# Graph layer 0: VectorE adds runs of equal targets before TensorE sums them per group

## The reference

```python
h = relu(layernorm(x))                                   # layer 0
agg = segment_sum(h[src], dst, 12500)
x = x + agg @ W_rel.T + b_rel + h @ W_root.T
h = relu(layernorm(x))                                   # layer 1
w = silu(edge_attr @ We1 + be1) @ We2 + be2              # 50 -> 128 -> 128 per edge
agg = segment_sum(h[src] * w, dst, 12500)
x = x + silu(agg @ Wn1 + bn1) @ Wn2 + bn2 + h
```

## Time and profile before

| | us |
|---|---|
| median of 3 runs | 4800.75 (4791.8 to 4805.88) |
| profiled execution | 4849.66, its span 4847.9 |
| POOL busy | 2970.8 (61%) |
| TensorE busy | 2418.4 (50%) |
| VectorE busy | 1276.0 (26%) |
| ScalarE busy | 479.4 (10%) |

### The profile page before, as it was taken

How to read it: one execution, slowest core, us unless ns; L and a number is a source line. 1 busy time by engine, 2 the same in 40 slices (tenths; PEclk the granted TensorE clock), 3 DMA queues, 4 the chain that set the end, 5 groups by cost and what they waited for, 6 DMA issues and landing times.

```text
span 4847.9 us, 35780 instructions
## 1 busy us (share of the span) xinstructions
PE 2418.4 (50%) x10938; PEld 1841.8 (38%) x10938; DVE 1276.0 (26%) x2181; ACT 479.4 (10%) x842; POOL 2970.8 (61%) x3135
## 2 busy tenths in 40 slices
PE   1332323232323232322447677777666777767667
PEld 0322322232222222222334445555454555544545
DVE  2511111111111111111323333333333333333334
ACT  3400000000000000000101111111111111111111
POOL 5366666666666666666465656666656666656662
PEclk9755556555656565655667767777767777767777
DMA  5222222222221222222222222222222222222222
GB/s 135 61 53 52 55 53 56 54 53 53 56 54 51 56 55 54 51 56 55 62 59 61 65 62 64 65 69 64 65 61 64 65 67 66 64 61 64 64 63 59
DMA packets 230579, 296.77 MB, mean 61 GB/s; under 512 B 68580, under 2 KB 160278, under 8 KB 230433
## 3 DMA queue, kind: packets, MB, share of 16 engines
q0 software_dynamic: 100096, 205.20, 16.8%
q10 hardware_dynamic: 61378, 60.59, 4.6%
q1 hardware_dynamic: 69086, 30.79, 2.4%
HBM read 269.87 MB, written 26.48 MB: 61 GB/s over the span
## 4 chain that ended last, share of the span: by engine, by line
another core or an unknown queue 44%; PE 26%; issue 17%; DVE 10%; DVEq 2%; ACT 1%; POOL 0%; DMA 0%; ACTq 0%; SPq 0%; POOLq 0%
PE seg_a L370 7%; PE seg_b L370 5%; PE ew_a L416 4%; PE ew_b L416 3%; DVE onehot L711 3%; PE hid_b L410 3%; PE hid_a L410 2%; DVE ew_a L817 2%; DVE rows L825 2%; DVE ew_b L817 1%; DVEq L719 1%; PE node L430 0%; DVE e_stats L625 0%; PE node L381 0%
## 5 line engine op out<-in xcount | busy, mean ns | idle before, releaser
L320 POOL DMA_INDIRECT rows<-h_rows,idx x3060 | 2905.5, 950 | 1783.2 <-issue 952.2
L370 PE MATMUL seg_a<-onehot,rows 128*128 128x128 f32 x3312 | 662.9, 358 | 1136.9 <-DVE onehot L711 445.2
L370 PEld LDWEIGHTS seg_a<-onehot,rows 128*128 128x128 f32 x3312 | 601.9, 268 | 1221.4 <-issue 934.2
L370 PE MATMUL seg_b<-onehot,rows 128*128 128x128 f32 x2944 | 572.5, 340 | 809.3 <-issue 576.9
L370 PEld LDWEIGHTS seg_b<-onehot,rows 128*128 128x128 f32 x2944 | 504.8, 249 | 855.7 <-issue 659.9
L711 DVE TENSOR_TENSOR onehot<-iota_ps,dst_rel 128x1536 f32<-128x1536 f32 (+1 forms) x278 | 461.3, 1659 | 1.0 <-DVE dst_rel L699 0.6
L817 DVE TENSOR_TENSOR ew_a<-ew_a,be_all 128x512 f32<-128x512 f32 x207 | 144.6, 699 | 1044.7 <-remote 703.2
L416 PE MATMUL ew_b<-we_sb,hidden 128*128 128x128 f32 x1472 | 289.3, 357 | 224.6 <-ACT hidden L578 177.1
L416 PEld LDWEIGHTS ew_b<-we_sb,hidden 128*128 128x128 f32 x1472 | 245.2, 252 | 406.5 <-ACT hidden L578 210.3
L416 PEld LDWEIGHTS ew_a<-we_sb,hidden 128*128 128x128 f32 x1664 | 268.6, 245 | 246.3 <-issue 169.0
L416 PE MATMUL ew_a<-we_sb,hidden 128*128 128x128 f32 x1664 | 310.8, 345 | 81.4 <-ACT hidden L578 55.2
(11 more groups left out here) (122 smaller groups left out, 1148.4 us busy)
## 6 DMA issues: line engine op xcount, KB each, us to landing
rows<-h_rows,idx POOLq DMA_INDIRECT x3060
ef_a<-ef_blocks ACTq DMA_DIRECT2D x70, 300.0 KB
node_work<-ef_blocks ACTq DMA_DIRECT2D x47, 300.0 KB
xs<-x SPq DMA_DIRECT2D x40, 256.0 KB
ys<-y_rows SPq DMA_DIRECT2D x26, 256.0 KB
out<-xs ACTq DMA_DIRECT2D x26, 256.0 KB
y_rows<-ys ACTq DMA_DIRECT2D x25, 256.0 KB
h_rows<-node_work ACTq DMA_DIRECT2D x23, 256.0 KB
```

The lines of the kernel that those rows point to most:

```text
L320: pool.indirect_dma_start(out=rows[:, u, t, :], out_offset=None, in_=table, in_offset=bass.IndirectOffsetOnAxis(ap=idx[:, j:j + 1], axis=0 ...
L370: mm = pe.matmul(seg[g % 2][:, 0:P], rows[:, u, t, :], onehot[:, g % 2, k * TB + t, :], start=(k == 0 and t == 0), stop=(last and t == TB ...
```

## The change

The edges are laid out in another order inside each group: partition p now holds 12 edges that are neighbours in the sorted list (8 in the last group), one in each of the group's tiles, instead of each tile holding 128 neighbours. The same order is used for the indices, the targets and the edge features. In layer 0 a partition's edges form runs of equal targets. For run r of a group VectorE multiplies the gathered rows by a 0/1 mask of the run (`picked`, line 834 of the new kernel) and adds them up over the group's tiles (`run_sum`, line 839). TensorE then multiplies three summed tiles by three one-hots (`run_hot`) per group. Three runs are handled in one turn over all edges; a partition with more would need further turns (`passes0`), and the number of turns is worked out at run time. POOL's gather of layer 0 now waits for the run sums (`s_sum`) and not for TensorE's. Layer 1 keeps its path, one-hots for each tile.

The run numbers and the run targets (`run_of`, `run_dst`) are worked out ahead of the phase that normalizes the nodes; the work on windows and passes and the clearing of `agg` move there too, and so does the load of `dst_sb` on SyncE's queue.

```diff
+R = 3
+MAX_RUNS = GB * TB
+RUN_STEPS = 2 * R
...
+        run_slots = onehot[:, :, :, :].rearrange("p a b c -> p (a b) c")
+        run_hot = [run_slots[:, R * k:R * k + R, :] for k in range(2)]
+        run_sum = [run_slots[:, R * (2 + k):R * (2 + k) + R, :] for k in range(2)]
+        picked = run_slots[:, 4 * R:4 * R + GB * TB, :]
...
             sp.dma_start(blk_sb[:, :, :], dst_blocks.rearrange("p (c e) -> p c e", e=BLOCK)).then_inc(s_blk, 16)
+            sp.dma_start(dst_sb[:, :, :], dst_cols.rearrange("p (k t) -> p k t", t=TB)).then_inc(s_dst, 16)
...
-                    hold(pool, s_seg[layer], i * G + (g + 1))
+                    if layer == 0:
+                        hold(pool, s_sum, runs_summed(i, g) - RUN_STEPS * G)
+                    else:
+                        hold(pool, s_seg[1], i * G + (g + 1))
...
+            def run_sums(i, g):
+                pe.wait_ge(s_sum, runs_summed(i, g))
+                for r in range(R):
+                    mm = pe.matmul(seg[g % 2][:, 0:P], run_sum[g % 2][:, r, :], run_hot[g % 2][:, r, :],
+                                   start=(r == 0), stop=(r == R - 1))
+                mm.then_inc(s_seg[0], 1)
...
+            def run_sums(i, it, g):
+                tiles = len(blocks_of(g)) * TB
+                first = g * GB
+                done = runs_summed(i, g) - RUN_STEPS
+                dve.wait_ge(s_sum, done)
+                v.tensor_tensor(run_mask[:, :, 0:tiles],
+                                dst_rel[:, bass.ds(it * U + first, tiles // TB), :].rearrange("p k t -> p (k t)")
+                                .unsqueeze(1).to_broadcast([P, R, tiles]),
+                                run_now[:, :].unsqueeze(2).to_broadcast([P, R, tiles]),
+                                ALU.is_equal).then_inc(s_mask, 1)
+                v.tensor_tensor(run_hot[g % 2], iota_ps[:, 0:P].unsqueeze(1).to_broadcast([P, R, P]),
+                                run_dst[:, bass.ds(it * G + g, 1), :].rearrange("p g r -> p (g r)").unsqueeze(2)
+                                .to_broadcast([P, R, P]), ALU.is_equal)
+                dve.wait_ge(s_mask, i * G + (g + 1))
+                for r in range(R):
+                    if r > 0:
+                        dve.wait_ge(s_sum, done + 2 * r)
+                    v.tensor_tensor(picked[:, 0:tiles, :],
+                                    rows[:, first:first + tiles // TB, :, :].rearrange("p k t f -> p (k t) f"),
+                                    run_mask[:, r, 0:tiles].unsqueeze(2).to_broadcast([P, tiles, P]),
+                                    ALU.mult).then_inc(s_sum, 1)
+                    dve.wait_ge(s_sum, done + (2 * r + 1))
+                    v.tensor_reduce(run_sum[g % 2][:, r, :], picked[:, 0:tiles, :].rearrange("p e f -> p f e"),
+                                         AX.X, ALU.add).then_inc(s_sum, 1)
...
                     for g in range(G):
+                        dve.wait_ge(s_rows[0][g], landed(i, g))
+                        run_sums(i, it, g)
                         if g > 0:
                             add_window(0, i, it, g - 1)
                         else:
                             add_window(0, i - 1, it - 1, G - 1)
-                        one_hot(it + (g + 1) // G, (g + 1) % G).then_inc(s_onehot, 1)
...
-                next_pass(p + 1)
+                next_turn(p * (2 * R + 7) + (2 * R + 2))
```

More of the change, by code:

```diff
@@ L351, in _ @@
             pe.wait_ge(s_ident, 1)
+            pe.wait_ge(s_run, 1)
+            pe.matmul(node[:, 0:P], scratch[:, 0:P], ident[:, :], start=True, stop=True).then_inc(s_run_max, 1)
             with pe.Fori(0, GROUPS // H_SETS) as k:
@@ L372, in segment_sum @@
                 if last:
[L373 removed]
+                    mm.then_inc(s_seg[1], 1)
             def node_update0(n, r):
@@ L437, in _ @@
             edge_weights(0, 0)
-            with pe.Fori(0, passes) as p:
+            with pe.Fori(0, passes1) as p:
                 with pe.Fori(0, ITERS) as it:
@@ L582, in _ @@
             load_ef(0, 1)
-            with act.Fori(0, passes) as p:
+            with act.Fori(0, passes1) as p:
                 with act.Fori(0, ITERS) as it:
@@ L637, in shift_of @@
                                        ALU.mult, ALU.mult).then_inc(s_done, 1)
+            dve.wait_ge(s_dst, 16)
+            dst_flat = dst_sb[:, :, :].rearrange("p k t -> p (k t)")
+            by_group = run_of.rearrange("p (i e) -> p i e", e=U * TB)[:, :, bass.ds(0, G, step=GB * TB)]
+            keep_start = scratch.rearrange("p (i e) -> p i e", e=U * TB)[:, :, bass.ds(0, G, step=GB * TB)]
+            v.tensor_scalar(dst_flat, dst_flat, 1.0, None, ALU.add)
+            v.memset(scratch, 1.0).then_inc(s_setup, 1)
@@ new lines, in _ @@
+            dve.wait_ge(s_setup, 13)
+            v.tensor_scalar(plan[:, 2:3], plan[:, 2:3], 1.0, None, ALU.add)
+            v.tensor_scalar(span[:, 1:2], span[:, 1:2], 0.0, 1.0 - LATE_STEPS, ALU.is_ge, ALU.mult).then_inc(s_setup, 1)
+            dve.wait_ge(s_setup, 14)
+            v.tensor_scalar(plan[:, 1:2], span[:, 1:2], float(LATE_STEPS), None, ALU.add)
+            dve.wait_ge(s_run_max, 1)
+            v.tensor_reduce(run_last[:, :], node[:, 0:P], AX.X, ALU.max).then_inc(s_setup, 1)
@@ L884 @@
     ef_pad[:N_EDGES] = edge_attr_50
-    src_cols = src_pad.reshape(-1, P).T
-    ef_cols = ef_pad.reshape(N_BLOCKS, BLOCK, D_EDGE).transpose(0, 2, 1)
+    order = []
+    for first in range(0, N_BLOCKS, U):
+        for g in range(0, U, GB):
+            tiles = min(GB, U - g) * TB
+            order.append((first + g) * BLOCK + np.arange(P * tiles).reshape(P, tiles).T.ravel())
+    order = np.concatenate(order)
+    src_cols = src_pad[order].reshape(-1, P).T
+    ef_cols = ef_pad[order].reshape(N_BLOCKS, BLOCK, D_EDGE).transpose(0, 2, 1)
     arrays = {
```

228 lines of the change are left out of this document (143 added, 85 removed).

## The result

The changed kernel takes 4909.7 us (median of 4 runs, 4906.3 to 4927.8) against 4802.3 us for the kernel before (4 runs): ratio 1.022, 95% interval 1.019 to 1.025. It is slower, by about 2%: 107 us, where the forecast said 358. The profiled execution took 4908.2 us, span 4906.4, 58.5 more than the profiled one of before, which was 47 us above its own median.

A forecast was written before the change was run, and what follows sets the result against it. It took POOL's gathers (85.0 us of a 97.7 us iteration) plus two stops, from slow TensorE, as the bound. 271 + 60 + 11 + 14 = +356 on 4850 gave 5206, less 49 about 5160 us; range 4600 to 5650.

The forecast's parts named there:

- the forecast's own case: Whole kernel: VectorE falls behind and POOL stops for it in layer 0; 4960 to 5320 us, chance 0.43.
- TensorE's part of the two stops goes: Layer 0 loop: 68 tiles become 18, so TensorE no longer causes POOL's two stops, 12.7 us an iteration.
- POOL's release: Layer 0 loop: POOL waits for VectorE's run sums in lock-step; 110 us an iteration instead of 97.7, +271 us.
- The second SBUF input costs 0.1 us a product and is left out: VectorE's products in layer 0: two SBUF inputs cost 0.1 us a product, judged from L765 against L759, and not counted.
- VectorE's own pace 77 us an iteration: Layer 0 loop: VectorE's work sums to 77 us an iteration in a quick state, under POOL's 85.0.
- rival B: Layer 0: the strided sum is dear as well, bound 3.4 us each; 5420 to 5730 us, chance 0.29.
- Iteration 0 +60: First layer 0 iteration: VectorE, already on the path, gains work and stalls; +60 us (40 to 90).
- Start +11: Before layer 0's loop: preparation moved ahead of the node phase, with late waits beside the first gathers; +11 us.
- next_turn +14: After layer 0's loop: run targets are worked out again on the path of the last node updates; +14 us.
- Rival A: Layer 0 loop: VectorE stays quick and POOL runs without stops, 86 us an iteration; 4616 us, chance 0.23.
- Rival C: Layer 0 loop: POOL's stops add up to the same as before, 97.7 us an iteration; 4886 us, chance 0.05.

The follow-up runs named there:

- e10: The kernel before with three unused products, both inputs in SBUF, behind each one-hot write of layer 0's iterations 1 to 22, slow set: 4938.2 us, ratio 1.019.
- e9: The changed kernel as it is, run again in a slow set: 4941.6 us, ratio 1.021.
- e2: The changed kernel with the sum reading 12 neighbouring elements instead of strided ones (wrong elements, same count), slow set: 4956.0 us, ratio 1.026.
- e3: The changed kernel with run mask and run numbers in PSUM and the product written to PSUM, summed there with the same stride: 5062.1 us, ratio 1.047.
- e4: The changed kernel with run mask and run numbers in PSUM, the product kept in SBUF but written across and read in order: 5159.2 us, ratio 1.067.
- e6: The kernel before with three unused products, second input in PSUM, behind each one-hot write of layer 0's iterations 1 to 22, quick set: 4000.2 us, ratio 1.000.
- e7: The kernel before with layer 0's sum matmuls (iterations 1 to 22) moving 32 one-hot columns instead of 128, quick set: ratio 0.9995.

## Why the prediction came out as it did

It had the direction and missed the size: +358 us forecast on the median, +107 measured, inside the wide range (4600 to 5650) but below the forecast's own case (4960 to 5320). By its own steps:

- *TensorE's part of the two stops goes.* Right: no `remote` idle time of POOL is left in layer 0. Of the 12.7 us that the stops cost, all were won.
- *POOL's release: VectorE falls behind whenever POOL gathers for longer than 11 us, 110 us an iteration, +271.* **This is the term that failed.** Measured: 100.3 us an iteration, +44 for the 22, no stop, and no wait of VectorE for itself that is late. The lock did not happen in the changed kernel.
- *The second SBUF input costs 0.1 us a product and is left out.* **This is the step that made it fail.** In its place the runs show 15.3 us of POOL's time an iteration (100.3 - 85.0), 0.85 us for each of 18 products. The forecast had looked at VectorE's operations (L765 against L759 in the earlier trace rows), but the one that pays is the gather. The gathers beside L765 wouldn't have warned either: each began within 0.02 us of it and was not held, which is no evidence on a gather that begins in the midst of a product. The one row of before that points at such gathers is the long one at the start of layer 1, by its end alone. By the Trainium skill's rule, which I priced at 2.8 us a group, the iteration would have been 85.0 + 6 x 2.8 = 102 us, and no gain left of the 12.7 us.
- *How the two hang together.* With the second input moved to PSUM (e1) a lock comes, at 108.3 us. The code of the changed kernel and of e1 differs in nothing else; they ran in different sets, but both slow sets of the changed kernel (e9 is the second) are free of it, e2 with its mask in SBUF is free of it in the very set of e1, and e3 and e4 with theirs in PSUM have it there. So the lock depends on that input. Its trigger was not what I had named: not the wait for an own semaphore but the pace of the instruction stream, 0.70 us an instruction and one stand of 22 us. That it is the held gathers themselves which protect is supported by e10 (stops down to a third) and is not shown.
- *VectorE's own pace 77 us an iteration.* Measured 86.2. The sum was mis-sized, 2.73 and 1.87 us for 1.75 and 1.2 (16.6 us an iteration); the rest of the group was cheaper, since the load of the window's place runs beside the last sum. A group takes 14.4 us, not 12.9. It stayed under POOL's 100.3, so rival B, whose mechanism was right at 0.6 of its bound, cost nothing in the loop, only 16.6 us in iteration 0.
- *Iteration 0 +60.* +51.6. *Start +11.* -15.0: VectorE's preparation (11.6 to 52.6 us) ran with quick waits, and the node phase, which had dragged beside the first gathers before, ended 3.5 us later than it had, while memset and window work of 17.7 us left its end (first one-hot at 161.60). *next_turn +14.* The step itself takes 13.7 us (2421.0 to 2434.7), but before, VectorE had waited 7.6 us for TensorE at this place: +5.8.
- *Rival A* said "POOL runs without stops"; it does, but with longer gathers. *Rival C*, "the iteration stays about where it was", was nearest in number (4886 us). That is luck: it had POOL's stops come back to the old sum, where in fact they went and held gathers took their place.

So of an iteration 12.7 us were won and 15.3 paid; iteration 0 and the end cost 57 us, the start gave 15 back.

## What to carry to other kernels

When work is moved to VectorE beside a GpSimd that issues gathers, count the instructions with two SBUF inputs and charge the gathers, not VectorE: 0.6 to 1.1 us here for each product of 1.75 us, more the earlier in the product the gather begins. One operand in PSUM takes the charge away. Then ask what the slower GpSimd had been good for: in the slow sets, removing the charge alone made the kernel slower (1.061 for 1.022). And look for the price of contention at the engine that is the bound, instruction by instruction and not in a mean, and see for each when it began. Rows in which the two begin together, as all 20 did in the loop of the kernel before, say nothing of the others.

## What the runs showed of the hardware that was not expected

- A gather that begins 0.07 us or more behind the start of a VectorE operation with two SBUF inputs ends 0.8 us behind that operation's end (all 363 products and all 20 L889 of the changed kernel's stretch). One that begins up to 0.02 us behind it (L765, 20 of 20), or ahead of it, takes 0.94 to 0.96.
- In the slow sets, while POOL gathers without a pause, instructions of VectorE and TensorE go in steps of 0.70 us (23 ns for VectorE's, 0.1 to 0.4 us for TensorE's otherwise), and in e1 VectorE stood still for 22 us at one place of the loop. No instruction fetch shows among the transfers between 379 and 2309 us of e1 and of the kernel before, so what is short there stays open. Nor was found what decides on the set: layer 1, the same code, took 2481 us in the kernel before and 1986 in e6 and e7, the iteration of layer 0 97.7 and 85.3.
- A sum that reads fp32 elements 512 bytes apart costs 2725 ns from SBUF, 1757 from PSUM, 1753 in order from SBUF; a product that writes them 48 bytes apart costs 2816 instead of 1755. The Trainium skill (SBUF — State Buffer, the box on cachelines) gives SBUF such a penalty for each new line; the runs agree for SBUF, and for PSUM show none in this read.
